# Gram products of the gated delta rule: odd chunks' keys expanded by VectorE, filler matmuls taken out, DRAM gathers and stores issued from two queues

## What is computed

```python
q = _l2norm(q) * SCALE; k = _l2norm(k)
beta = sigmoid(x @ b_w.T + b_bias + beta_bias) * 2.0
g = -exp(A_log) * softplus(x @ a_w.T + dt_bias)
def step(S, inp):
    S = S * exp(g_t)[..., None, None]
    mem = einsum('bhk,bhkv->bhv', k_t, S)
    delta = (v_t - mem) * b_t[..., None]
    S = S + einsum('bhk,bhv->bhkv', k_t, delta)
    return S, einsum('bhk,bhkv->bhv', q_t, S)
```

## Time and profile before

| | us |
|---|---|
| median of 3 runs | 3573.55 |
| lowest, highest | 3564.75, 3577.44 |
| the profiled execution | 3556.71 |
| its span, first to last instruction | 3554.9 |

### The profile page before, as it was taken

One profiled execution on the slowest core, in us unless ns is written; L12 is line 12 of the kernel. 1 busy time (PEld: TensorE's weight loads), 2 busy tenths in 40 slices (PEclk: granted clock), 3 DMA queues, 4 the chain that ended last, 5 costly groups with the idle time before them and its releaser, 6 DMA issues.

```text
span 3554.9 us, 30862 instructions
## 1 busy us (share of the span) xinstructions
PE 2762.9 (78%) x10802; PEld 1650.7 (46%) x10802; DVE 2312.5 (65%) x2269; ACT 1242.4 (35%) x1663; POOL 1023.5 (29%) x516
## 2 busy tenths in 40 slices
PE   5888805888588999998747768778796778688887
PEld 2333704666345799986312223223332323376665
DVE  3555274666564566665489998999899997622222
ACT  3333000000122255543345544544544332333333
POOL 0000802333111200032054645545454553021111
PEclk9888957999798999999979979988998999899998
DMA  5332911000411466652134434544344456000000
GB/s 175 104 98 80 81 17 45 0 0 0 166 70 63 163 241 236 244 189 92 48 94 125 137 106 143 139 116 127 121 136 113 125 158 217 27 1 12 12 5 19
DMA packets 230911, 359.46 MB, mean 101 GB/s; under 512 B 88432, under 2 KB 106864, under 8 KB 225168
## 3 DMA queue, kind: packets, MB, share of 16 engines
q1 hardware_dynamic: 224816, 328.67, 33.2%
q0 software_dynamic: 5120, 16.78, 1.3%
q10 hardware_dynamic: 864, 12.58, 0.8%
HBM read 304.26 MB, written 65.27 MB: 104 GB/s over the span
## 4 chain that ended last, share of the span: by engine, by line
PE 44%; DVE 29%; issue 14%; ACT 7%; DMA 3%; SPq 1%; POOL 1%; PEldq 0%; PEld 0%; DVEq 0%; POOLq 0%; ACTq 0%
DVE arena L1157 12%; DVE arena L1164 6%; PE psum L2060 5%; PE psum L1680 4%; PE psum L1681 3%; PE psum L2164 2%; PE psum L2158 2%; DVE tmpA L1999 2%; PE psum L1423 2%; PE psum L1425 2%; PE psum L1424 2%; PE psum L387 2%; PE psum L394 1%; PE psum L1668 1%; PE psum L1669 1%
## 5 line engine op out<-in xcount | busy, mean ns | idle before, releaser
L607 POOL TENSOR_TENSOR arena<-arena 128x1024 f32<-128x1024 f32 x256 | 629.1, 2459 | 672.4 <-DVE arena L1164 383.6
L1573 PE MATMUL psum<-arena,cst 128*128 128x512 f32 x1024 | 547.6, 666 | 290.8 <-DVE arena L1164 257.4
L1157 DVE TENSOR_TENSOR_SCAN arena<-psum,arena 128x512 f32<-128x512 f32 x512 | 596.0, 1204 | 29.9 <-POOL arena L607 19.6
L800 ACT ACTIVATE psum<-arena,negA 128x512 f32<-128x512 f32 x512 | 351.3, 690 | 644.9 <-DVE arena L1157 644.5
L1573 PEld LDWEIGHTS psum<-arena,cst 128*128 128x128 f32 x1024 | 193.8, 205 | 631.2 <-DVE arena L1164 396.1
L1761 POOL TENSOR_TENSOR arena<-arena,cst 128x1024 f32<-128x1024 f32 x96 | 200.0, 2098 | 690.8 <-DMA v_tok<-arena 355.1
L1164 DVE TENSOR_TENSOR arena<-arena 128x1024 f32<-128x1024 f32 x256 | 371.0, 1449 | 0.0
L1518 PE MATMUL psum<-arena 128*128 128x512 f32 x512 | 239.0, 613 | 31.5 <-DVE arena L1127 19.9
L1680 PE MATMUL psum<-r 128*128 128x512 f32 x512 | 209.9, 410 | 33.4 <-ACT arena L888 23.6
L2060 PE MATMUL psum<-arena 128*128 128x512 f32 x384 | 191.9, 658 | 49.8 <-DMA arena<-in_x 25.2
L1271 DVE TENSOR_TENSOR r<-arena,r 128x512 fp32r<-128x512 f32 x64 | 44.2, 692 | 266.7 <-ACT r L893 266.7
(11 more groups left out here) (272 smaller groups left out, 5337.2 us busy)
## 6 DMA issues: line engine op xcount, KB each, us to landing
arena<-bc_scr SPq DMA_DIRECT2D x256, 512.0 KB, 4.9
arena<-w_exp SPq DMA_DIRECT2D x23, 1408.0 KB, 6.1
arena<-in_inw SPq DMA_DIRECT2D x32, 512.0 KB, 4.7
arena<-in_gu SPq DMA_DIRECT2D x24, 512.0 KB, 5.4
x_scr<-arena SPq DMA_DIRECT2D x23, 512.0 KB, 6.6
arena<-in_dn SPq DMA_DIRECT2D x23, 512.0 KB, 6.9
arena<-x_scr SPq DMA_DIRECT2D x23, 512.0 KB, 7.6
o_scr<-arena SPq DMA_DIRECT2D x23, 512.0 KB, 5.8
```

The costliest lines, as they stand in the source:

```text
L607: nc.gpsimd.tensor_tensor(dB[:, k % 4], du[:, j:j + 2], BC[:, k % RING, 0].unsqueeze(1).broadcast_to([P, 2, T]), ALU.mult).then_inc(s["db_ ...
L800: nc.scalar.activation(psum[:, 2 + t], dt[:, b % 2, j + t], ACT.Exp, scale=negA2[:, at:at + 1]).then_inc(s["da_ok"], 1)
L1157: v.tensor_tensor_scan(dB[:, k % 4, t], psum[:, 2 + t], dB[:, k % 4, t], 0.0, ALU.mult, ALU.add).then_inc(s["sc"], 1)
L1573: ins = mm(psum[:, t], ident, dB[:, k % 4, t], start=(n == 0), stop=(n == NS - 1))
```

## The change

- VectorE gets the function `expand` ahead of its Gram loop and expands the odd chunk's keys into KX[:, 1] there, with a semaphore of its own (kxd_ok), before it evicts the two chunks of the iteration. GpSimd expands the even chunks only. TensorE waits for one semaphore or the other. VectorE's waits for g_out and vt_out move ahead of the loop.
- The three fillers per chunk are gone from the Gram loop. The 16 ahead of it stay.
- ACT issues the eight gathers of the first part of m_scr and three of the eight of the second; SP stores both parts, the second without having gathers to issue before it (semaphore m_out2), and issues the other five.
- The t_scr stores are issued by SP (four) and ACT (four); SP waits for all eight and reloads as before.

```diff
+        GRAM_PART = ((0, 12), (12, 16))
+
+        def gather_m(queue, h, qa, qb):
+            queue.dma_start(PM[16 * h + qa:16 * h + qb].rearrange("p j (l u) i -> p (j l) (u i)", u=2),
+                            m_scr[16 * h:16 * h + 16].rearrange("j (l q r) -> q (j l) r", l=TL, q=16)[qa:qb]
+                            ).then_inc(s["m_in"], 16)
+
+        def scatter_t(queue, h):
+            queue.dma_start(t_scr[16 * h:16 * h + 16].rearrange("j (l q r) -> q (j l) r", l=TL, q=16),
+                            PT[16 * h:16 * h + 16].rearrange("p j (l u) i -> p (j l) (u i)", u=2)
+                            ).then_inc(s["t_out"], 16)
...
-            for i, (qa, qb) in enumerate(((0, 12), (12, 16))):
+            for i, (qa, qb) in enumerate(GRAM_PART):
                 sp.wait_ge(s["g_ev"], 2 + 2 * qb)
                 sp.dma_start(m_scr.rearrange("p (l t) -> p l t", l=TL)[:, :, 32 * qa:32 * qb],
-                             MT[:, :, 32 * qa:32 * qb]).then_inc(s["m_out"], 16)
-                sp.wait_ge(s["m_out"], 16 * (i + 1))
-                for h in range(8):
...
+                             MT[:, :, 32 * qa:32 * qb]).then_inc(s[("m_out", "m_out2")[i]], 16)
+                if i == 1:
+                    sp.wait_ge(s["m_out2"], 16)
+                    for h in range(5):
+                        gather_m(sp, h, qa, qb)
             sp.wait_ge(s["pt_ok"], 1)
-            for h in range(8):
...
+            for h in range(4):
+                scatter_t(sp, h)
             sp.wait_ge(s["t_out"], 128)
             sp.dma_start(MT.rearrange("p l t -> p (l t)"), t_scr).then_inc(s["t_in"], 16)
...
             with pool.Fori(0, NCH // 2) as half:
-                for u in range(2):
-                    c = 2 * half
-                    pool.wait_ge(s["g1_mm"], c + u + 1)
-                    expand(KX[:, u], KQ[:, 0], c + u, s["kx_ok"])
+                c = 2 * half
+                pool.wait_ge(s["g1_mm"], c + 1)
+                expand(KX[:, 0], KQ[:, 0], c, s["kx_ok"])
...
+            act.wait_ge(s["m_out"], 16)
+            for h in range(8):
+                gather_m(act, h, *GRAM_PART[0])
+            act.wait_ge(s["m_out2"], 16)
+            for h in range(5, 8):
+                gather_m(act, h, *GRAM_PART[1])
+            act.wait_ge(s["pt_ok"], 1)
+            for h in range(4, 8):
+                scatter_t(act, h)
...
             with dve.Fori(0, NCH // 2) as half:
+                c = 2 * half
+                dve.wait_ge(s["g1_mm"], c + 2)
+                expand(KX[:, 1], KQ[:, 0], c + 1, s["kxd_ok"])
                 for u in range(2):
-                    c = 2 * half
                     dve.wait_ge(s["g1_mm"], 2 + c + u + 1)
...
-                    pe.wait_ge(s["kx_ok"], c + u + 1)
+                    pe.wait_ge(s[("kx_ok", "kxd_ok")[u]], half + 1)
                     pe.wait_ge(s["g_ev"], c + u + 1)
                     for l in range(TL):
-                        if l in (2, 4, 6):
-                            pace(2, 1)
                         ins = mm(psum[:, u, l * 32:(l + 1) * 32], KX[:, u, l], KQ[:, :, l, ds((c + u) * CH, CH)], start=True, stop=True)
```

More of the change, by code:

```diff
@@ L230, in build @@
         f_dh f_ds f_hh f_hl xh_ok xl_ok tw_in th_ok tl_ok ab_ok sum_mm sc_ok tq_ok t_g t_u t_s
-        t_up t_act t_dn ach2 dch2 dch3""".split()
+        t_up t_act t_dn ach2 dch2 dch3 kxd_ok m_out2""".split()
         names += [f"f_gin{i}" for i in range(4)] + [f"f_din{i}" for i in range(4)] + ["cw_in0", "cw_in1"] + [f"bc_in{q}" for q in range(2)]
@@ L249, in build @@
                 ("wl_ok", "bc_mm", 4 * B), ("bx_mm", "g_mm", 8 * B), ("bxh_ok", "ab_mm", 2 * B), ("bxl_ok", "gt_a", 2 * B),
-                ("bg_mm", "gt_d", 2 * B), ("bu_mm", "qs_ok", NQKV * B), ("bs_ok", "kx_ok", NCH), ("ba_ok", "kx2_ok", NCH),
+                ("bg_mm", "gt_d", 2 * B), ("bu_mm", "qs_ok", NQKV * B), ("bs_ok", "kx_ok", NCH // 2), ("ba_ok", "kx2_ok", NCH),
                 ("bt_mm", "qx_ok", NCH), ("bah_ok", "tx_ok", NCH), ("bal_ok", "ax_ok", NCH), ("bd_mm", "ks_mm", NCH),
@@ L1718, in _ @@
                                  ).then_inc(s["v_in"], 16)
-            for i, (qa, qb) in enumerate(((0, 12), (12, 16))):
+            for i, (qa, qb) in enumerate(GRAM_PART):
                 sp.wait_ge(s["g_ev"], 2 + 2 * qb)
                 sp.dma_start(m_scr.rearrange("p (l t) -> p l t", l=TL)[:, :, 32 * qa:32 * qb],
-                             MT[:, :, 32 * qa:32 * qb]).then_inc(s["m_out"], 16)
-                sp.wait_ge(s["m_out"], 16 * (i + 1))
-                for h in range(8):
-                    sp.dma_start(PM[16 * h + qa:16 * h + qb].rearrange("p j (l u) i -> p (j l) (u i)", u=2),
-                                 m_scr[16 * h:16 * h + 16].rearrange("j (l q r) -> q (j l) r", l=TL, q=16)[qa:qb]
-                                 ).then_inc(s["m_in"], 16)
+                             MT[:, :, 32 * qa:32 * qb]).then_inc(s[("m_out", "m_out2")[i]], 16)
[3 more added lines that the diff above has]
+                        gather_m(sp, h, qa, qb)
             sp.wait_ge(s["pt_ok"], 1)
-            for h in range(8):
-                sp.dma_start(t_scr[16 * h:16 * h + 16].rearrange("j (l q r) -> q (j l) r", l=TL, q=16),
-                             PT[16 * h:16 * h + 16].rearrange("p j (l u) i -> p (j l) (u i)", u=2)
-                             ).then_inc(s["t_out"], 16)
+            for h in range(4):
+                scatter_t(sp, h)
             sp.wait_ge(s["t_out"], 128)
@@ L1956, in _, with expand @@
             dve.wait_ge(s["ab_used"], 2 + 2 * B)
+            def expand(dst, src, i, done):
+                v.tensor_tensor(dst.rearrange("p l (h j) -> p l h j", h=8),
+                                src[:, :, ds(i * CH, CH)].unsqueeze(2).broadcast_to([P, TL, 8, CH]),
+                                bmask.unsqueeze(1).unsqueeze(3).broadcast_to([P, TL, 8, CH]), ALU.mult).then_inc(done, 1)
+            dve.wait_ge(s["bc_used"], 4 + 4 * B)
+            dve.wait_ge(s["qs_ok"], NQKV * B)
+            dve.wait_ge(s["g_out"], 16 * B)
+            dve.wait_ge(s["vt_out"], 16 * B)
             with dve.Fori(0, NCH // 2) as half:
+                c = 2 * half
+                dve.wait_ge(s["g1_mm"], c + 2)
+                expand(KX[:, 1], KQ[:, 0], c + 1, s["kxd_ok"])
                 for u in range(2):
-                    c = 2 * half
                     dve.wait_ge(s["g1_mm"], 2 + c + u + 1)
@@ L1967, in _ @@
             ch.link(v.tensor_tensor(V, V, bcol.unsqueeze(3).broadcast_to([P, TL, NCH, DV]), ALU.mult))
-            dve.wait_ge(s["g_out"], 16 * B)
-            dve.wait_ge(s["vt_out"], 16 * B)
             ch.link(v.tensor_copy(PT, dl16.unsqueeze(2).broadcast_to([P, CH, 2 * TL, CH])))
@@ L1980, in _ @@
             dve.wait_ge(s["t_in"], 16)
[L1982 to L1985, removed]
             v.memset(S[:, 0], 0.0).then_inc(s["s_ok"], 1)
```

## The result

The changed kernel takes 3586.98 us (median of 11 runs, 3573.86 to 3594.99), the kernel before 3571.93 us in the runs beside them (11, 3564.75 to 3583.00): a ratio of 1.0034, 95% interval 1.0020 to 1.0047, 15 us slower. 3586 us had been forecast, from 12.3 us on top of a median of before of 3573.55. The profiled execution took 3584.66 us around a span of 3581.5.

A forecast was written before the change was run, and what follows sets the result against it. The path was VectorE's waits for Gram matmuls, last m_scr gather and t_scr reload, with its own work between. Inverse start +21 us and t_scr stores -8.7 gave +12.3 on 3573.55: 3586 us, range 3572 to 3602.

The forecast's parts named there:

- Fillers, clock at 0.50 from the third chunk on, loop's end at 468.8: Gram loop on TensorE: without fillers the clock falls, 3.5 us per chunk, loop ends at 468.8, 34.5 us later.
- First part by ACT costs nothing: First m_scr part: ACT is idle, so its issues delay nothing; store lands at 446.8, eight gathers at 472.3.
- Second store 476: Second m_scr store on a free queue: issued at 468.5, 7.5 us under way, landed at 476.
- Last gathers 13.5 us: Last eight m_scr gathers, five by SP and three by ACT: 13.5 us instead of 17.8, bounds 11.1 and 17.8.
- the slack: VectorE's wait for the last gathers falls from 20.2 to about 7 us, taking back 13.5 of the loop's 34.5 us.
- Stores 18 us: Eight t_scr stores, four each by SP and ACT: 18 us instead of 26.7, saving 8.7 us.
- One feed for both queues: Rival: clock falls, gathers and t_scr stores keep their present pace, stores +0; 3599 us; chance 0.27.
- Two independent queues: Rival: clock falls, last gathers take 11.1 us and t_scr stores 13.4; +5.3 us, 3579 us; chance 0.17.
- the lower bound of 13.4: Lower end for the eight t_scr stores, in us, if both queues run independently; the upper end was 26.7.
- VectorE's expansions cost nothing: Gram loop: VectorE's odd-chunk expansions add 19.7 us, hidden in its 65.6 us wait; excluding GpSimd's also costs nothing.
- Sum +12.3: Whole kernel: +21 us for the later start of the inverse, -8.7 us for the t_scr stores, together +12.3 us.

The follow-up runs named there:

- the kernel with the longer lead: The changed kernel with the three fillers per chunk put back and 22 instead of 16 fillers ahead of the Gram loop; ratio 0.9977 to the kernel before.
- the fillers-back kernel: The changed kernel with the three fillers per chunk put back in the Gram loop, the rest as changed; ratio 1.0074 to the kernel before.
- the kernel with two queues only: The kernel before with gathers and stores divided between SP and ACT, fillers in, GpSimd expanding all chunks; ratio 0.9962, median 3542.52 us.

## Why the prediction was right, step by step

The estimate of the loop rests on line 2164 at both clocks. That its 1.97 us at 616.39 belong to the high clock was taken for granted there; this window of the kernel before shows it:

```profile
616.00:618.00 2.00, 2.00 (x18) 1.74 (x16) 1.08 (x2) 0.31 (x1) 0.00 (x0) 1.00 0.00 0
```

- **Fillers, clock at 0.50 from the third chunk on, loop's end at 468.8.** 0.50 from 360.5 on, V's product at 467.71. The fall came sooner, in the first chunk, and a chunk took 3.4 us (467.7 less 359.0, over 32) instead of 3.5. The two errors go opposite ways, by some 2 and 3 us, so that the end was met within 1 us is partly luck. Line 2164 at the low clock is the same instruction. The cause is shown: the loop without fillers stands at 0.50 whoever expands, and with fillers and GpSimd's expansions at 1.00. The Trainium skill (TensorE: Matmul & The Clock Gate, "HAM oscillation — how this bites in real kernels") tells of a clock that falls through long idle gaps of the engine. This loop contradicts it: the clock fell also where TensorE's idle time ahead of the loop was 0.18 us (GpSimd expands all), and it stayed at 0.50 through 107 us in which TensorE was busy for 106.6 (360.5 to 467.5 in the changed kernel).
- **First part by ACT costs nothing.** Issued 440.51 and landed 446.50, forecast 440.8 and 446.8. That it costs nothing was wrong for the slow loop that the prediction itself forecast: SP alone is through with the part by 460.0 there and its second store lands in 3.5 us, while ACT's issues run to 468.3, past that store's issue. By the traces the division of the gathers costs 2.3 us (130.6 and 133.0 to the inverse), little more than the spread.
- **Second store 476**, landed 476.01, issued 0.7 us sooner than forecast and 8.2 instead of 7.5 us under way. The reason was right too, the last gathers in the way; where SP issued them alone at the slow clock, it was 3.5 us.
- **Last gathers 13.5 us**: 15.3, inside the bounds of 11.1 and 17.8, nearer the middle. This is the term that was somewhat off. Inverse at 491.32 for 489.5; the slack gave back 10.6 us instead of 13.5.
- **Stores 18 us**: 17.8. One feed for both queues (26.7) is refuted. Two independent queues are not: SP's four issues took 11.12 us, half of the 22.66 us of its eight before, and ACT's four took 13.39 beside them. What fails in the lower bound of 13.4 is that it halves the last landing too: the time from the end of the last issue to the reload was 4.1 us before and is 4.4 now. So 18, chosen between two bounds, met the number without this working. The Trainium skill (DMA: Bandwidth & Descriptors, "Issuing engines are not separate DMA queues") says that a second issuer saves only the issuing time, usually small. The trace agrees with the first half, and not with the second: 22.66 of the 26.7 us were issuing time, and 9.3 of them are saved. From "usually small" the prediction took that the stores would stay near 26.7, although its own row has the 22.66 us. For the first part's gathers a second issuer saved next to nothing (65 GB/s instead of 62).
- **VectorE's expansions cost nothing.** Wrong in a detail that the working had in hand. Port exclusion was weighed per pair, but not at the start, where both engines begin at once and TensorE has no buffer ahead. It makes the first chunk 1.1 us late and costs up to 3 us by the inverse here, and with the fillers in place it went with the loss of the clock in eight of ten executions.
- **Sum +12.3**: +13.8 by the trace, 15 by the medians. The time lies in the range's middle, partly since errors cancel: 1 us off at the loop's end, 3 the other way after it. That 3586 was met within 1 us is luck as well: the step was 2.7 us larger than forecast, and the median of before 1.6 us lower in the runs beside the changed kernel.

What stays open is why the clock fell at 399 us in the kernel with the longer lead, where TensorE's own work did not change. The fall comes as the V gathers end (a share of 1.58 just before it, 0.05 just after), but they end inside the loop before as well (1.75 in 404 to 408, 0.00 from 412 on), and there the clock stays at 1.00. It also stays open what puts an execution of the fillers-back kernel into one group or the other. Neither was pursued further.

## What to carry to other kernels

Before taking out work that nobody reads, read the granted clock at the stretch, and find the remaining instruction form in the trace at both clocks: that gave the time of a chunk within 3%, and with some luck the loop's end within 1 us. Test the parts of a mixed change one by one; here a real gain of two queues (ratio 0.9962 alone) was hidden under a larger loss from the clock (1.0075 for the missing fillers alone). A second issuing queue paid here where one engine was inside its issues for most of the stage and the DMA share was low (0.44, 0.36), and brought next to nothing where the share was above 1.2; read both before dividing transfers. And when two engines hold each other up, look first at the moment when both start at once.

## What was not expected of the hardware

- With three fillers per chunk the clock in this loop mostly keeps to the level that it has. It stays at 1.00 if it is there (TensorE busy 44.65 of 46 us; one profiled execution fell at 399 us) and at 0.50 if it has fallen, although TensorE is then busy without pause (46.00 of 46). Which one an execution gets can differ: 3547 and 3550 us against 3585 to 3596 for one kernel.
- ACT issues the same transfers more slowly than SP: medians of 4.10 and 3.48 us for the t_scr stores issued side by side. The eight gathers of the first part took ACT 21.8 us to issue in the changed kernel, and SP 17.4 (before without fillers) and 20.6 (before). In the kernel with two queues only, SP's median was 4.00 for the small gathers of the second part, issued beside ACT's, so an issue's length also tells what is queued.
- A VectorE instruction of 1.23 us, begun 0.09 us earlier, made an expansion on GpSimd take 2.92 us in place of 1.9.
